# Second batch's values as three one-pass products, maxima split by GpSimd, joint gate logits

## What is computed

```python
x = x + cross_attention(layernorm(x), ctx, ctx, mask)   # 16 heads of 16, 4096 keys a batch
x = x + retention(layernorm(x))                          # 4 heads, keys 64, values 128
x = x + experts(layernorm(x))                            # 8 experts, softmax gate, weights under 0.1 dropped

# cross attention
q = query @ w_q.T + b_q; k = key @ w_k.T + b_k; v = value @ w_v.T + b_v
scores = where(mask, -inf, q @ k.T / 4)
out = softmax(scores) @ v @ w_o.T + b_o
```

## Time and profile before

| | |
|---|---|
| median of 3 runs | 207.33 us (207.29 to 207.42) |
| profiled execution | 208.21 us, of which span 206.3 us |
| TensorE busy | 194.6 us, 94% |
| VectorE busy | 142.8 us, 69% |
| ScalarE busy | 108.0 us, 52% |
| GpSimd busy | 70.1 us, 34% |
| granted TensorE clock, mean | 0.995 |

### The profile page before, as it was taken

The page is one execution under the profiler, slowest core; times in us unless marked ns, Lnnn a source line. Parts: engine busy times, 40 slices in busy tenths (PEclk is TensorE's granted clock), DMA queues, the critical chain, the costliest instruction groups (busy, mean ns, idle before and its releaser), DMA issues.

```text
span 206.3 us, 5923 instructions
## 1 busy us (share of the span) xinstructions
PE 194.6 (94%) x2446; PEld 133.2 (65%) x2446; DVE 142.8 (69%) x297; ACT 108.0 (52%) x230; POOL 70.1 (34%) x72
## 2 busy tenths in 40 slices
PE   8998999889999989998999999999999999998991
PEld 8566654446566647565666755477778887877780
DVE  3482578997396484698889636279676486996893
ACT  3235667758586575786979896243416333201200
POOL 8407894355073040068949341001003013010000
PEclk9999999999999999999999999999999999999997
DMA  5979965328119586066000000000000000000001
GB/s 180 289 200 271 322 155 145 99 65 219 45 41 243 114 289 263 3 219 195 5 5 5 3 0 3 0 0 5 0 0 0 3 0 2 3 2 27 25 30 35
DMA packets 15827, 18.10 MB, mean 88 GB/s; under 512 B 2656, under 2 KB 14896, under 8 KB 15792
## 3 DMA queue, kind: packets, MB, share of 16 engines
q1 hardware_dynamic: 14496, 17.30, 28.5%
q10 hardware_dynamic: 1296, 0.34, 0.8%
HBM read 9.81 MB, written 0.52 MB: 50 GB/s over the span
## 4 chain that ended last, share of the span: by engine, by line
PE 73%; DVE 9%; DMA 6%; ACT 3%; SPq 3%; issue 3%; POOL 0%; DVEq 0%; ACTq 0%
PE bank L904 11%; PE bank L981 11%; PE bank L999 11%; PE bank L861 4%; PE bank L847 4%; DVE cneg L1828 4%; PE bank L1199 3%; PE bank L1049 3%; PE bank L1088 3%; DMA ctxT<-in_ctxT 3%; PE bank L1219 3%; PE bank L1092 3%; PE bank L1089 3%; PE bank L1221 2%; PE bank L1220 2%
## 5 line engine op out<-in xcount | busy, mean ns | idle before, releaser
L1828 DVE TENSOR_REDUCE cneg<-bank 128x1 f32<-128x896 f32 x64 | 67.8, 1089 | 24.9 <-PE bank L904 24.9
L1507 ACT ACTIVATE prob<-bank 128x512 f32<-128x512 f32 x112 | 64.3, 600 | 15.9 <-PE bank L981 14.6
L981 PE MATMUL bank<-qstack,kstack 100*32 100x256 bf16 x896 | 43.8, 273 | 1.7 <-ACT prob L1507 1.2
L904 PE MATMUL bank<-kstack,qstack 97*32 97x448 bf16 x512 | 36.9, 354 | 2.6 <-DVE cneg L1828 0.9
L981 PEld LDWEIGHTS bank<-qstack,kstack 100*32 100x32 bf16 x896 | 23.7, 96 | 20.4 <-ACT prob L1507 4.0
L999 PE MATMUL bank<-prob,vals 128*32 128x256 f32 x448 | 34.8, 381 | 0.0
L605 POOL TENSOR_TENSOR nw<-nw,halves 128x2 f32<-128x2 f32 (+1 forms) x10 | 8.2, 825 | 63.5 <-DVE nw L1711 45.2
L904 PEld LDWEIGHTS bank<-kstack,qstack 97*32 97x32 bf16 x512 | 12.4, 95 | 9.9 <-DVE cneg L1828 4.4
L999 PEld LDWEIGHTS bank<-prob,vals 128*32 128x32 f32 x448 | 12.8, 109 | 4.6 <-issue 2.9
L1219 PE MATMUL bank<-exp_high,xn_high 128*128 128x512 f32 (+1 forms) x36 | 14.3, 396 | 0.0
L847 PE MATMUL bank<-ctxT,wk 128*128 128x448 f32 x32 | 13.8, 552 | 0.4 <-DMA ctxT<-in_ctxT 0.4
(11 more groups left out here) (182 smaller groups left out, 320.3 us busy)
## 6 DMA issues: line engine op xcount, KB each, us to landing
kstack<-kpart SPq DMA_DIRECT2D x21, 224.0 KB
w_late<-in_w_ret SPq DMA_DIRECT2D x1, 1536.0 KB, 6.6
mask_all<-in_mask SPq DMA_DIRECT2D x2, 512.0 KB, 4.3
ctxT<-in_w_exp SPq DMA_DIRECT2D x1, 1024.0 KB, 5.3
kpart<-in_w_exp SPq DMA_DIRECT2D x1, 1024.0 KB, 9.1
ctxT<-in_ctxT SPq DMA_DIRECT2D x2, 448.0 KB, 5.0
ctxT<-in_ctxT SPq DMA_DIRECT2D x1, 896.0 KB, 8.1
qstack<-acc SPq DMA_DIRECT2D x12, 64.0 KB, 3.6
```

The lines of the kernel that those rows point to most:

```text
L904: mm = pe.matmul(out[j4:j4 + COLS, :], qstack[0:MROW + 1, h, b, qt * P + j4:qt * P + j4 + COLS], kstack[0:MROW + 1, b, h, half_ * HC:(half ...
L981: mm = pe.matmul(out[j4:j4 + COLS, hh * NQ:(hh + 1) * NQ], kstack[0:KROWS, b, h, kt * P + j4:kt * P + j4 + COLS], qstack[0:KROWS, h, b, :] ...
L1507: act.activation(prob[:, n % PROBS, :], bank[:, c.score_bank(u, jj), :], ACT.Exp).then_inc(c["prob_ready"], 1)
L1828: dve.tensor_reduce(cneg[:, st % 2, i:i + 1], bank[:, pair:pair + 2, 0:HC], AXXY, ALU.max, negate=True).then_inc(c["max_read"], 1)
```

## The change

Three things are changed on the fast path.

First, the second batch's values. GpSimd casts the context of the second batch and the weights to fp32r (`ctx_high`, over the first batch's context, and `wv_high`, over `wq`), and subtracts to get the low parts (`wv_low`, `ctx_low`, in place). TensorE then makes three fp32r products in place of each f32 one: high by high, high by low and low by high.

Second, the maxima of the stages 1 to 6 are split by GpSimd (`cut_maxima`); VectorE keeps those of stage 0 and 7.

Third, the gate logits of the two tiles of a batch lie side by side in the bank, and VectorE reads both at once.

```diff
+            def cut_maxima(st):
+
+                mp = mpart[:, st % 2, :, :, :]
+                mv = cneg[:, st % 2, :].rearrange("p (t h) -> p t h", t=QT)
+                pool.wait_ge(*only.at("max_read", TILES * (st + 1)))
+                pool.wait_ge(*only.at("max_cut", st))
+                if st >= 2:
+                    pool.wait_ge(*only.at("rows_turned", st - 1))
+                pool.tensor_copy(mp[:, :, 1, :], mv).then_inc(s["cut_chain"], 1)
+                pool.wait_ge(s["cut_chain"], 3 * st - 2)
+                pool.tensor_tensor(mrest[:, :, :], mv, mp[:, :, 1, :], ALU.subtract).then_inc(s["cut_chain"], 1)
+                pool.wait_ge(s["cut_chain"], 3 * st - 1)
+                pool.tensor_copy(mp[:, :, 2, :], mrest[:, :, :]).then_inc(s["cut_chain"], 1)
+                pool.wait_ge(s["cut_chain"], 3 * st)
+                pool.tensor_tensor(mp[:, :, 3, :], mrest[:, :, :], mp[:, :, 2, :], ALU.subtract).then_inc(only["max_cut"], 1)
+
             def between_cuts(i):
 
                 if i < 2:
-                    pool.wait_ge(*only.at("max_cut", 6 + i))
+                    cut_maxima(5 + i)
                 else:
                     pool.wait_ge(s["at_ready"], QT)
 
+            def split_context():
+
+                pool.wait_ge(*only.at("v_evac", NVP))
+                pool.wait_ge(*only.key("k_taken", 2))
+                pool.wait_ge(s["q_taken"], 3)
+                pool.wait_ge(*only.at("ctx_loaded1", 16))
+                pool.tensor_copy(ctx_high[:, :, :], ctxT[:, 1, :, :]).then_inc(s["split"], 1)
+                pool.tensor_copy(wv_high[:, :, :], wv[:, :, :]).then_inc(s["split"], 1)
+                pool.wait_ge(s["split"], 2)
+                pool.tensor_tensor(wv_low[:, :, :], wv[:, :, :], wv_high[:, :, :].bitcast(F32), ALU.subtract).then_inc(s["split"], 1)
+
+            def split_context_rest():
+
+                pool.wait_ge(*only.key("k_taken", 3))
+                for i in range(KIN):
+                    pool.tensor_tensor(ctx_low[:, i, :], ctxT[:, 1, i, :], ctx_high[:, i, :].bitcast(F32), ALU.subtract).then_inc(s["split"], 1)
+
             with pool.If(fast > 0):
                 pool.wait_ge(s["q_cut"], 3)
-
-                pool.wait_ge(*only.at("max_cut", 2))
+                split_context()
+
+                cut_maxima(1)
                 keys_cut(only, 2)
-                pool.wait_ge(*only.at("max_cut", 3))
+                split_context_rest()
+                cut_maxima(2)
                 keys_cut(only, 3)
-
-                pool.wait_ge(*only.at("max_cut", 4))
+                cut_maxima(3)
                 stream_and_bias()
+                cut_maxima(4)
 
...
+            def split_values(blocks, out):
+
+                pe.wait_ge(s["split"], CTX_PARTS)
+                for k in blocks:
+                    some, keys_ = out[:, (k - blocks[0]) * D:(k - blocks[0] + 1) * D], slice(k * P, (k + 1) * P)
+                    for i in range(KIN):
+                        pe.matmul(some, ctx_high[:, i, keys_], wv_high[:, i, :], start=(i == 0), stop=False)
+                        pe.matmul(some, ctx_high[:, i, keys_], wv_low[:, i, :], start=False, stop=False)
+                        mm = pe.matmul(some, ctx_low[:, i, keys_], wv_high[:, i, :], start=False, stop=(i == KIN - 1))
+                mm.then_inc(only["v_ready"], 1)
...
-SIDES = [("ro", 0), ("ro", 1), ("logit", 0), ("logit", 1), ("ro", 2), ("ro", 3), ("bias", 0),
-         ("logit", 2), ("logit", 3), ("bias", 1)]
+SIDES = [("ro", 0), ("ro", 1), ("logit", 0), ("ro", 2), ("ro", 3), ("bias", 0), ("logit", 1), ("bias", 1)]
...
-                    out = side("logit", t)
+                    b, i = divmod(t, QT)
+                    if i == 0:
+                        side("logit", b)
+                    out = bank[:, SIDE, i * 2 * NE:(i + 1) * 2 * NE]
...
+                if not c.loop and st > 1 and i == 0:
+                    dve.wait_ge(*only.at("max_cut", st - 1))
                 dve.tensor_reduce(cneg[:, st % 2, i:i + 1], bank[:, pair:pair + 2, 0:HC], AXXY, ALU.max, negate=True).then_inc(c["max_read"], 1)
...
-                    for t in tiles:
-                        n_ = SIDE_AT["logit", t] + 1
-                        dve.wait_ge(s["side_ready"], n_)
-                        post(dve.tensor_tensor(glog[:, t, :], bank[:, SIDE, 0:NE], gb_row[:, :], ALU.add))
-                        dve.tensor_tensor(glog[:, t, :], bank[:, SIDE, NE:2 * NE], glog[:, t, :], ALU.add).then_inc(s["side_taken"], 1)
+                    n_ = SIDE_AT["logit", b] + 1
+                    parts = bank[:, SIDE, 0:QT * 2 * NE].rearrange("p (t i e) -> p t i e", t=QT, i=2)
+                    dve.wait_ge(s["side_ready"], n_)
+                    post(dve.tensor_tensor(glog[:, both, :], parts[:, :, 0, :], gb_row[:, :].unsqueeze(1).to_broadcast([P, QT, NE]), ALU.add))
+                    dve.tensor_tensor(glog[:, both, :], parts[:, :, 1, :], glog[:, both, :], ALU.add).then_inc(s["side_taken"], 1)
```

More of the change, by code:

```diff
@@ L786, in _ @@
                 stream_and_bias()
+                pool.sem_inc(s["split"], CTX_PARTS)
                 split_late(lambda i: None)
@@ L871, in values @@
                 value_blocks(c, 0, range(2 * n, min(2 * n + 2, KB)), bank[:, c.value_bank(n), :])
+            def split_values(blocks, out):
[7 more added lines that the diff above has]
+                mm.then_inc(only["v_ready"], 1)
             def later_values(c, n):
                 pair = take_pair(c, "v", n)
-                value_blocks(c, 1, range(4 * n, min(4 * n + 4, KB)), bank[:, pair:pair + 2, :].rearrange("p b k -> p (b k)"))
+                out = bank[:, pair:pair + 2, :].rearrange("p b k -> p (b k)")
+                blocks = range(4 * n, min(4 * n + 4, KB))
+                if c.loop:
+                    value_blocks(c, 1, blocks, out)
+                else:
+                    split_values(blocks, out)
             def max_tile(c, m):
@@ L1208, in logits @@
                     taken("n3", t)
-                    out = side("logit", t)
+                    b, i = divmod(t, QT)
+                    if i == 0:
+                        side("logit", b)
+                    out = bank[:, SIDE, i * 2 * NE:(i + 1) * 2 * NE]
                     for c in range(KIN):
                         both = gate_parts[:, c, :, :].rearrange("p i e -> p (i e)")
-                        for i, part in enumerate((xn_high, xn_low)):
-                            mm = pe.matmul(out[:, 0:2 * NE], part[:, c, t * P:(t + 1) * P], both, start=(c == i == 0), stop=(c == i == KIN - 1))
-                    mm.then_inc(s["side_ready"], 1)
+                        for h, part in enumerate((xn_high, xn_low)):
+                            mm = pe.matmul(out, part[:, c, t * P:(t + 1) * P], both, start=(c == h == 0), stop=(c == h == KIN - 1), skip_group_check=True)
+                    if i == QT - 1:
+                        mm.then_inc(s["side_ready"], 1)
                 def split_product(out, t, c, experts):
@@ L1827, in take_maximum @@
                 dve.wait_ge(*c.at("max_ready", m + 1))
+                if not c.loop and st > 1 and i == 0:
+                    dve.wait_ge(*only.at("max_cut", st - 1))
                 dve.tensor_reduce(cneg[:, st % 2, i:i + 1], bank[:, pair:pair + 2, 0:HC], AXXY, ALU.max, negate=True).then_inc(c["max_read"], 1)
-                last = m
-                if not c.loop and st > 1 and i == 0:
-                    st, last = st - 1, m - 1
-                elif i < TILES - 1 or not c.loop and 0 < st < STAGES - 1:
+                if i < TILES - 1 or not c.loop and 0 < st < STAGES - 1:
                     return
-                dve.wait_ge(*c.at("max_read", last + 1))
+                dve.wait_ge(*c.at("max_read", m + 1))
+                if not c.loop and st:
+                    dve.wait_ge(*only.at("max_cut", st))
                 new_maximum(c, st)
```

16 lines of the change are left out of this document (10 added, 6 removed).

## The result

| | before | after |
|---|---|---|
| median | 207.29 us (206.86 to 209.13, 7 runs) | 209.18 us (208.11 to 210.58, 7 runs) |
| profiled execution | 208.21, span 206.3 | 210.37, span 208.5 |
| granted TensorE clock, mean | 0.995 | 0.992 |

The ratio of the runs is 1.0096, with a 95% interval of 1.0054 to 1.0138: the change makes the kernel slower by 1.1 to 2.9 us. Executions 1.5% or more above the fastest of their kernel are left out of the ratios (four of the six of e3, three of the twelve of e12, one of the twelve of e13), but not out of medians and ranges.

The account below looks back on a forecast made before the run. TensorE, busy 94% of the span, was taken as the bound. The terms -1.44 + 2.6 + 0.8 + 0 - 0.74 = +1.2 us, applied to the 207.33 us median, gave 208.5 us; range 207.6 to 209.5, 8 in 10 206.6 to 210.2.

Parts of the forecast that it names:

- a fall of TensorE's clock: Sign that the prediction is wrong, if seen in the changed kernel's profile; the sum had no term for it.
- Step A: Second batch's two values calls on TensorE: 42 one-pass matmuls take 5.0 us against 6.44, -1.44 us (-1.2 to -1.6).
- Step B: Stage 2's maxima split waits behind two GpSimd subtractions, so TensorE stands still at these rows: +2.6 us (+1.9 to +3.5).
- the cover: Stage 1's maxima split on GpSimd done at 43.2, TensorE wants it at 44.17: hidden, with 0.9 us to spare.
- The price by the rule that doubles the small operations: GpSimd's four small operations at twice VectorE's time: 1.6 us, stall 3.1, sum +1.7; the forecast used the profile's rows instead.
- Step C: Stage 3's rows on SyncE issued late behind the constants, after the shifted third key split: +0.8 us (0 to +1.3).
- Step D: VectorE's four operations less per stage in the loop, some 0.6 us: 0 gained, at best -0.2 near 44 us.
- Step E: Joint gate logits, second batch: TensorE needn't wait for VectorE's read between two tiles, -0.74 us (-0.5 to -0.9).
- The clock: Rival: the stall lets TensorE's clock fall to 1.2 GHz for 1 to 3 us of work: 209.5 to 211.5; 12%.
- The stop without a releaser: TensorE's unexplained 0.85 us stop at 96 us in the attention loop; its place moves as matmuls are added.
- the first rival: Stall comes, but the rows aren't late or the 0.85 us stop goes: 207.7 or 207.8, both 206.9; 17%.

Follow-up runs that it names:

- e3: The changed kernel with GpSimd's cut of stage 2's maxima between the two subtractions for the context's low part; 212.43 us, ratio 1.0144.
- e12: e9 with the maxima cut by VectorE as before, GpSimd splitting only context and weights; 208.62 us, ratio 1.0049.
- e13: e9 with ten matmuls, their result not read, ahead of TensorE's wait for stage 2's rows; 206.49 us, ratio 0.9962.
- e2: e1 with the transfer of stage 3's rows also ahead of the late constants on SyncE's queue; 207.47 us, ratio 1.0034.
- e1: The changed kernel with GpSimd's cut of stage 2's maxima ahead of the two subtractions for the context's low part; 210.39 us, ratio 1.0145.
- e4: The changed kernel with ten matmuls, their result not read, ahead of TensorE's wait for stage 2's maxima; 210.04 us, ratio 1.012.
- e5: The kernel before with the joint gate logits alone; 205.70 us, ratio 0.9925.
- e7: The changed kernel without the three-product values; GpSimd cuts only the maxima, and the logits are joint; 205.76 us, ratio 0.9959.
- e9: The changed kernel with SyncE's eleven constant loads issued ahead of the wait for stage 2's rows, GpSimd's order unaltered; 208.31 us, ratio 1.0067.
- e10: e8 with the float32 values of before, no split of context and weights on GpSimd; 205.45 us, ratio 0.9905.
- e11: The kernel before with the eleven constant loads issued ahead of the wait for stage 2's rows, nothing else; 206.88 us, ratio 0.9962.
- e8: e1 with SyncE's eleven constant loads issued ahead of the wait for stage 2's rows; 204.58 us, ratio 0.9879.

## Why the prediction was right, and where it was not

The forecast was 208.5 us and slower; the median is 209.18, within its range of 207.6 to 209.5. The direction, the stall, and the reason for it were right. But the prediction named a fall of TensorE's clock as a sign that it is wrong, and the clock fell. That the sum came near is in part luck: of the measured differences +1.47 (the clock), +0.74 (the loop's rest) and +0.63 (the start) had no term in it, and where it had +0.8 for late rows the stretch became 1.20 us shorter. By its steps:

- **Step A, the values.** Forecast -1.44 us; the two calls gained 0.65 and 0.50, so -1.15, just under the lower bound of 1.2. The rate was right: 24 matmuls at 0.117 us. The term left out is the start of each call, 2.99 us from the first value matmul to the next sums in e2, 0.18 over 24 x 0.117. It stood among the bounds as 0.1 per call and should have been in the sum.
- **Step B, the stall.** Forecast +2.6, measured 2.33, made as written: two subtractions of 2.07 (forecast 2.1), then four operations 0.27 apart. TensorE asked at 59.15, 0.8 us later than before, most of it from a load at the start, and GpSimd was done at 61.4, 0.5 later than forecast. e1 shows the cause: with the cut ahead, the stretch is 6.68 as before. GpSimd's cut of stage 1 began at 42.94, 0.8 us later than forecast: 0.6 because the query splits ended at 38.88 in this execution, and 0.2 because the first casts and the subtraction were slower. It was done at 43.96, TensorE turned these rows at 44.79, and the cover held. The price by the rule that doubles the small operations, 1.6 us for the four, did not come: they took 1.1, with 0.19 to 0.21 each, and only two of them have two inputs.
- **Step C, the late rows.** Forecast +0.8; in the changed kernel nothing of it shows. The step failed because it had two sizes wrong. TensorE was late not by the stall alone but by 1.47 us of clock more. And SyncE's list from the first copy of the third key split to the last constant took 12.0 us, not the 12.8 of before, so it ended at 74.93 and not at 75.6; even without the clock the rows, ready at about 75.5, would have found it free. The mechanism is real, but it varies with the execution, and where it shows it is larger than forecast: with the stall gone a stop of 3.23 us (e1), without the low clock 3.16 (e4). The prediction took the transfer as 2.43 us; in e1 it took 3.4 and in e4 4.3. A constant of 768 KB was issued 2 us ahead of it in e1, but in the kernel before one was issued 2.5 us ahead too, with 348 GB/s moving from 72 to 74 us, so what makes it slower is not shown.
- **Step D, VectorE's relief.** Forecast 0; e5 and e7 agree within what their runs can tell. But the text saw only relief, and e12 shows that with the subtractions on GpSimd the old cut on VectorE would itself have been held for 2.3 us.
- **Step E, the logits.** Forecast -0.74; the last stretch of the table shortens from 70.8 us to between 69.9 and 70.4 in every kernel that has it, and the wait for `glog` is gone.
- **The clock.** Given 12% as a rival with +1 to +3 us, it did happen: +1.47 in the profile of after, +1.53 by the stretches of e9 and e13. This is the step that was judged wrongly: the sum put the fall at nothing. A stop of 2.33 us was followed by it here, against the 0.85 us of before that left the clock alone.
- **The stop without a releaser.** 0.85 us before, 1.67 in the profile of after, 0.2 to 0.6 in others and absent in e4, e5, e10, e11 and e13, always between 94 and 101 us. It moved with the program, as the first rival said, but against the forecast's interest: +0.8 in this execution.

What remains open. The stretch behind stage 3's rows is 7.99 before and 8.12 in e5, with a stop of 0.7 and 1.2 us put down to ScalarE's `prob`; in e5 that ended at 76.46 and TensorE went on at 77.40, so it wasn't this. The profiled execution of e5 took 206.94 us and its other runs 205.54 to 206.10, so it may be that it comes and goes. What makes it, what makes the stop without a releaser, and why e5 gains 0.8 us more than its last stretch shows, was not settled.

## What to carry to other kernels

An idle engine's queue is not free: when work is moved to it, list what now stands ahead of each small piece that the bound engine asks for, and put the small piece first, since a cut of 1.1 us behind 4.1 us of subtractions cost 3.7 us here (e9 against e8), 1.5 of them by the clock. A stall hides the next one; remove it alone and the next is paid (e1 was no faster than the kernel it mended), so follow the late engine's products through every queue, the DMA issuer's too, and mend them together. Loads that nobody waits for belong where the issuing queue stands idle for another reason, neither ahead of a small urgent transfer nor so late that their bytes run beside one.

## What was not expected of the hardware

- The length of a stop did not tell whether the clock falls. A stop of TensorE of 2.33 us was followed by a stretch at 1.2 GHz from 62.1 to 65.5, worth about 1.5 us; the filler in that stop kept the clock at 1.00 (e13). A stop of 1.67 us in e12, with one of 0.50 a microsecond later, was followed by such a stretch too, from 61.8 to 65.2. But the stop of 2.83 us in e2 and the one of 1.67 us at 97.5 us in after were followed by windows at 1.00.
- A transfer of 8 KB took 2.4, 3.1, 3.4, 4.3 and 4.9 us in before, e3, e1, e4 and e2. The 4.9 lay amid 377 to 390 GB/s; but the 2.4 lay amid 348 and then 121 GB/s, so the traffic beside it does not tell the time alone.
- An instruction of VectorE on eight elements took 2.00 us in place of 0.17 while GpSimd ran one subtraction of 896.
